# Vision tower on one core: prologue order, value stages of two attentions, and the class token's scale

## The reference

```
# tokenizer: 128 images, a 9x9 grid of 14x14x3 patches in 9 windows of 3x3 patches
pe   = conv(pixel_values, conv_w)                     # 81 patches x 256
red  = mean of pe over the 9 patches of a window
q    = layernorm(red)*g+b @ la_wq ; k, v = layernorm(pe)*g+b @ la_wkv
local= red + softmax(q k * scale) v @ la_proj_w + la_proj_b       # one query, 9 keys
cls  = class_emb + softmax(gq gk * scale) gv @ ga_proj_w + ga_proj_b   # 9 windows as keys
h    = concat(local @ mod_w + mod_b, cls)             # 10 tokens an image
# attention 0 (16 heads of 16, 10 tokens, two scores masked), mixture of experts,
# attention 1 (causal over 10 tokens, scores clipped), low-rank block:
h = h + attention0(layernorm(h)) ; h = h + experts(layernorm(h))
h = h + attention1(layernorm(h)) ; h = h + lowrank(layernorm(h))
```

## Time and profile before

| | us |
|---|---|
| median of 3 runs | 852.29 (847.16 to 853.2) |
| the profiled execution | 849.13 |
| its span | 847.4 |
| mean granted clock of PE, share of full | 0.931 |
| busy: PE, DVE, ACT, POOL | 729.8, 535.9, 358.6, 396.5 |

### The profile page before, as it was taken

How to read it: one execution, slowest core, us unless ns; L and a number is a source line. 1 busy time by engine, 2 the same in 40 slices (tenths; PEclk the granted TensorE clock), 3 DMA queues, 4 the chain that set the end, 5 groups by cost and what they waited for, 6 DMA issues and landing times.

```text
span 847.4 us, 13115 instructions
## 1 busy us (share of the span) xinstructions
PE 729.8 (86%) x4399; PEld 630.6 (74%) x4399; DVE 535.9 (63%) x1253; ACT 358.6 (42%) x904; POOL 396.5 (47%) x272
## 2 busy tenths in 40 slices
PE   2879999999999999996846755999999999595668
PEld 2869998988989887553645754999999999354666
DVE  1578787777777777678999653222222223679956
ACT  3465666656656555532010131444444444162131
POOL 4565767667576661548564202333334332147410
PEclk9899999999999999999958865999999999597999
DMA  8532222222222020000020047799989980400001
GB/s 257 174 91 81 86 87 86 81 60 76 87 86 84 4 100 1 0 1 0 1 100 1 26 174 298 239 339 325 332 331 331 330 327 28 160 0 2 0 1 63
DMA packets 34489, 102.76 MB, mean 121 GB/s; under 512 B 3624, under 2 KB 12152, under 8 KB 27000
## 3 DMA queue, kind: packets, MB, share of 16 engines
q1 hardware_dynamic: 31832, 94.84, 32.6%
q0 software_dynamic: 2592, 7.10, 2.2%
HBM read 95.75 MB, written 6.17 MB: 120 GB/s over the span
## 4 chain that ended last, share of the span: by engine, by line
PE 69%; DVE 20%; POOL 3%; DMA 2%; issue 2%; ACT 1%; SPq 1%; POOLq 1%; DVEq 0%; ACTq 0%
PE banks L1581 12%; PE banks L1589 11%; PE banks L287 10%; PE banks L289 10%; PE banks L288 10%; PE banks L294 6%; PE banks L300 4%; DVE a_prod L1158 4%; PE banks L1260 4%; DVE a_o L1469 2%; DVE a_s L1393 2%; DVE banks L1393 1%; DVE w_raw L1402 1%; PE banks L1290 1%; PE banks L1919 1%
## 5 line engine op out<-in xcount | busy, mean ns | idle before, releaser
L401 POOL TENSOR_TENSOR x_lo<-xraw,x_hi 128x640 fp32r<-128x640 f32 x81 | 129.3, 1603 | 109.8 <-ACT x_hi L395 109.8
L287 PE MATMUL banks<-wc_hi,x_hi 128*128 128x256 f32 x405 | 121.9, 301 | 17.9 <-POOL x_lo L401 12.6
L1679 ACT ACTIVATE hid<-banks,b 128x128 f32<-128x128 f32 x216 | 79.3, 367 | 110.0 <-PE banks L1581 110.0
L288 PE MATMUL banks<-wc_lo,x_hi 128*128 128x256 f32 x405 | 116.5, 288 | 0.0
L289 PE MATMUL banks<-wc_hi,x_lo 128*128 128x256 f32 x405 | 116.4, 287 | 0.0
L287 PEld LDWEIGHTS banks<-wc_hi,x_hi 128*128 128x128 f32 x405 | 79.5, 196 | 20.4 <-issue 12.9
L1838 DVE TENSOR_TENSOR res<-banks,xb 128x256 f32<-128x256 f32 x27 | 11.5, 425 | 127.2 <-PE banks L1589 127.2
L288 PEld LDWEIGHTS banks<-wc_lo,x_hi 128*128 128x128 f32 x405 | 79.7, 197 | 1.8 <-issue 0.2
L289 PEld LDWEIGHTS banks<-wc_hi,x_lo 128*128 128x128 f32 x405 | 79.3, 196 | 0.0
L424 DVE BATCH_NORM_STATS2 stats<-banks 128x6 f32<-128x256 f32 x81 | 34.6, 427 | 69.7 <-ACT pe_sb L418 69.0
L418 ACT ACTIVATE pe_sb<-banks 128x256 f32<-128x256 f32 x81 | 31.0, 383 | 111.8 <-PE banks L289 111.8
(11 more groups left out here) (298 smaller groups left out, 1778.5 us busy)
## 6 DMA issues: line engine op xcount, KB each, us to landing
w_raw<-in_w SPq DMA_DIRECT2D x28, 1024.0 KB, 6.7
xraw<-in_x_main SPq DMA_DIRECT2D x27, 768.0 KB
w1more<-in_w SPq DMA_DIRECT2D x13, 1024.0 KB, 5.8
w2more<-in_w SPq DMA_DIRECT2D x13, 1024.0 KB, 8.2
xraw<-in_x_rest SPq DMA_DIRECT2D x27, 114.0 KB
yl<-y_rows SPq DMA_DIRECT2D x2, 1028.0 KB, 7.1
a_w<-in_qkv_w SPq DMA_DIRECT2D x2, 768.0 KB, 5.4
x_rows<-w_raw SPq DMA_DIRECT2D x5, 256.0 KB, 2.0
```

The costliest lines, as they stand in the source:

```text
L287: pe.matmul(dst, a[0], b[0], start=start, stop=False)
L288: pe.matmul(dst, a[0], b[1], start=False, stop=False)
L401: pool.tensor_tensor(x_lo[:, i % RING_X, :], xraw[:, k].rearrange("p c b -> p (c b)"), x_hi[:, i % RING_X, :], ALU.subtract).then_inc(sem( ...
L1679: act.activation(hid[:, s % 2, fc, :], bank(fc % 2, 0, P), ACT.Gelu, bias=b1[:, bass.ds(e * FC + fc, 1)]).then_inc(sem("gelu_made"), 1)
```

## The change

- SP issues the first third of the first window, `vecs`, `wkv`, and then the other two thirds; `rows` moves behind them and is counted with the other weights (112 becomes 128). DVE's wait before the bias columns asks for `vecs` and `wkv` alone.
- PE's product of the bias columns moves from behind patch 5 to behind patch 1, the turn from 7 to 4; ACT's split of the weights from 8 to 5; DVE scales them behind `measure(1)`. POOL's first inverse root moves from behind `x_lo` 7 to 6. Normalizing patches 0 and 1 and turning patch 0 move ahead of the end of the loop (ACT at i = 10, 11; PE ahead of the last `conv`).
- Attention 0's class token: the maximum of its scores is kept in PSUM; DVE's product of score row 7 moves ahead of the wait for the projected class token; DVE subtracts the mean before POOL's inverse root is there, and ACT multiplies by the root alone.
- Value stages: ACT writes the values again with the key as the inner axis (`spread_values`: layer 0 in one instruction of 2560 elements behind the exponentials, layer 1 one of 256 elements for each tile). DVE's product reads these and writes in the same order, all through one slot. POOL folds a row of more than 5 keys: a second instruction adds the upper keys onto the lower ones (5 of 5 rows in layer 0, rows 6 and 8 in layer 1), and PE sums 5 keys instead of 10 (4 or 5 instead of 7 and 9).
- h is added by PE (one more identity product behind `project_o`'s), ACT copies the sum to h, and `add_o` keeps only the statistics.

```diff
@@ lower_scores
+            top_score = smax[:, :] if n < NW else bank(6, C, C + H8)
+            link(dve.tensor_reduce(top_score, by_head(sc), AX, ALU.max))
+            dve.tensor_tensor(by_key(sc), by_key(sc), over_keys(top_score), ALU.subtract).then_inc(sem("score_made"), 1)
@@ act_end
-            norm_x(act, 0, 9)
+            act.wait_ge(sem("rstd_made"), batch_of("attention 0", 3)[0] + 1)
+            act.wait_ge(sem("a_turned"), NW - 1)
+            act.activation(a_xn[:, NW % 2, :], agg[:, :], ACT.Identity, scale=rstd[2][:, NW:NW + 1]).then_inc(sem("a_xn_made"), 1)
@@ dve_end
             pool_sums(dve, link, 0, 5)
+            row_product(dve, 0, 7)
             dve.wait_ge(sem("proj_done"), NW + 1)
...
-            shift_of(dve, *batch_of("attention 0", 3))
+            dve.tensor_scalar(agg[:, :], h_at(NW), mv[2][:, NW, 0:1], None, ALU.subtract).then_inc(sem("nmr_made"), 1)
             pool_sums(dve, link, 0, 6)
-            for t in range(7, T):
+            row_sum(dve, link, 0, 7)
+            for t in range(8, T):
@@ value products
+        def kept_keys(layer, t):
+            n = keys(layer, t)
+            return (n + 1) // 2 if n > HALF else n
+        def fold_pool_values(pool, layer, t):
+            n, m = keys(layer, t), kept_keys(layer, t)
+            slot = pool_slot(layer, t)
+            return pool.tensor_tensor(slot[:, 0:(n - m) * C], slot[:, 0:(n - m) * C], slot[:, m * C:n * C], ALU.add)
+        def values_by_channel(n=T):
+            return a_prod[:, 1, :].rearrange("p (c s) -> p c s", s=T)[:, :, 0:n]
+        def dve_values(dve, layer, t):
...
+            return dve.tensor_tensor(a_prod[:, 0, 0:n * C].rearrange("p (h d s) -> p h d s", h=H16, s=n),
+                                     values_by_channel(n).rearrange("p (h d) s -> p h d s", d=D16),
+                                     p_t.unsqueeze(2).broadcast_to([P, H16, D16, n]), ALU.mult)
@@ pool_attention
+                if folded(layer, t):
+                    pool_values(pool, layer, t).then_inc(sem("unfolded"), 1)
+                    pool.wait_ge(sem("unfolded"), NW + 1 + made)
+                    fold_pool_values(pool, layer, t).then_inc(sem("a_pool_values_made"), 1)
@@ pe_attention: turn_o, project_o
-                ns, slot = keys(layer, t), pool_slot(layer, t)
+                ns, slot = kept_keys(layer, t), pool_slot(layer, t)
...
-                mm_rows(pe, bank(6 + t % 2), a_oT[:, t % 2, :], wo, 0, C).then_inc(sem("a_o_done"), 1)
+                for c in range(CH):
+                    pe.matmul(bank(6 + t % 2), a_oT[:, t % 2, c * P:(c + 1) * P], wo[:, c, :], start=(c == 0), stop=False)
+                pe.matmul(bank(6 + t % 2), ident[:, :], h_at(t), start=False, stop=True).then_inc(sem("a_o_done"), 1)
@@ act_attention
+        def spread_values(act, layer, a, b):
+            act.wait_ge(sem("a_qkv_made"), seen(layer, "qkv_made", 2 * b))
+            act.activation(values_by_channel()[:, :, a:b].rearrange("p c s -> p s c"), a_qkv[:, a:b, 2 * C:3 * C], ACT.Copy)\
+               .then_inc(sem("a_values_spread"), 1)
+        def copy_h(act, layer, t):
+            act.wait_ge(sem("a_o_done"), seen(layer, "o_done", t + 1))
+            act.activation(h_at(t), bank(6 + t % 2), ACT.Copy).then_inc(sem("a_h_made"), 1)
@@ add_o
-            dve.wait_ge(sem("a_o_done"), seen(layer, "o_done", t + 1))
-            dve.tensor_tensor(h_at(t), bank(6 + t % 2), h_at(t), ALU.add).then_inc(sem("a_h_made"), 1)
@@ sync
+            load_x(sp, 0, 0, first=True)
+            sp.dma_start(vecs[:, :], d["vecs"]).then_inc(sem("wkv_loaded"), 16)
+            sp.dma_start(wkv_raw[:, :, :], two("la_wkv")).then_inc(sem("wkv_loaded"), 16)
+            for g in range(1, NP // GRP):
                 load_x(sp, 0, g, first=True)
-            sp.dma_start(rows[:, :], d["rows"].broadcast_to([P, len(ROWS) * C])).then_inc(sem("wkv_loaded"), 16)
+            sp.dma_start(rows[:, :], d["rows"].broadcast_to([P, len(ROWS) * C])).then_inc(sem("tok_w_loaded"), 16)
@@ vector, prologue
-            dve.wait_ge(sem("wkv_loaded"), 48)
+            dve.wait_ge(sem("wkv_loaded"), 32)
```

More of the change, by code:

```diff
@@ L1215, in pool_attention @@
                     pool.wait_ge(sem("a_o_turned"), seen(layer, "o_turned", POOL_VALUES[layer][i - 2] + 1))
-                value_products(pool, layer, t, pool_slot(layer, t)[:, 0:n * C].rearrange("p (s h d) -> p s h d", s=n, d=D16))\
-                    .then_inc(sem("a_pool_values_made"), 1)
+                made = sum(folded(0, q) for q in POOL_VALUES[0]) * layer + sum(folded(layer, q) for q in POOL_VALUES[layer][:i + 1])
+                if folded(layer, t):
+                    pool_values(pool, layer, t).then_inc(sem("unfolded"), 1)
+                    pool.wait_ge(sem("unfolded"), NW + 1 + made)
+                    fold_pool_values(pool, layer, t).then_inc(sem("a_pool_values_made"), 1)
+                else:
+                    pool_values(pool, layer, t).then_inc(sem("a_pool_values_made"), 1)
             if layer == 0:
@@ L1350, in act_attention @@
                         copy_qkv(act, 1, t - 1)
-                    if t >= 4:
-                        row_exponent(act, SCORED[t - 4])
+                        spread_values(act, 1, t - 1, t)
+                    if t >= 5:
+                        row_exponent(act, SCORED[t - 5])
                 copy_qkv(act, 1, T - 1)
-                for t in SCORED[T - 4:]:
+                for t in SCORED[T - 5:T - 2]:
+                    row_exponent(act, t)
+                spread_values(act, 1, T - 1, T)
+                for t in SCORED[T - 2:]:
                     row_exponent(act, t)
@@ L2141, in _ @@
             link = Chain(dve, "link")
-            for i in range(EARLY_KEYS):
+            for i in range(2):
                 measure(dve, i)
-            early_variances(dve, 0)
             dve.wait_ge(sem("kvb_done"), 1)
@@ L2150, in _ @@
                    .then_inc(sem("wkv_scaled"), 1)
[L2151 removed]
+            for i in range(2, EARLY_KEYS):
                 measure(dve, i)
[L2153 removed]
+            early_variances(dve, 0)
             dve.wait_ge(sem("wkv_hi_made"), CH)
@@ L2157, in _ @@
                    .then_inc(sem("wkv_lo_made"), 1)
-            measure(dve, 8)
+            for i in range(EARLY_KEYS, 7):
+                measure(dve, i)
+            shift_of(dve, 0, 0, EARLY_KEYS)
+            for i in range(7, NP):
+                measure(dve, i)
             late_variances(dve, 0)
-            measure(dve, 9)
+            measure(dve, NP)
+            dve.wait_ge(sem("tok_w_loaded"), 128)
             tile_stats(dve, "class", 0, rows[:, 3 * C:4 * C])
```

88 lines of the change are left out of this document (45 added, 43 removed).

## The result

The changed kernel took 821.9 us (median of 4 runs, 819.8 to 825.99) beside 850.87 of the kernel before on the same chip: a ratio of 0.9674, 95% interval 0.9641 to 0.9707. The forecast was 819 (811 to 831) and faster. The profiled execution took 819.8 us, 29.3 less than the 849.1 of before; the sum of the forecast was 30.6.

What follows compares the result with a forecast made beforehand. PE is nearly full in rounds and experts, so only thin stretches can shrink: 5.2 (prologue) + 3.4 (class token) + 12 (attention 0) + 10 (attention 1) = 30.6 off 849.1 gives 818.5, stated as 819 us, range 811 to 831.

Steps and rivals of the forecast that it cites:

- Prologue, 5.2: Before the rounds: reordered steps start PE's first projection at 46.5 instead of 51.7; gain 5.2 us, from 2 to 8.
- The sum over POOL's queue: Prologue: from the first root at 29.2, splits, waits, roots, class shift and split product add up to 46.5.
- PE's stop before patch 7: Prologue: DVE's split of the weights (2.7 us) ahead of `measure(5)` holds patch 7 to about 31.5.
- Class token, 3.4: Attention 0's class token: early subtraction lets ACT start at about 398 instead of 401.2; gain 3.4 us, from 1 to 5.6.
- The rival of the held subtraction: Class token: POOL's next product makes the subtraction wait 3.4 us, so that gain is gone; 822, chance 0.05.
- Attention 0, 12: Attention 0's values: faster DVE products, folds and fewer PE products end the stage at 476.5, not 488.57; gain 12 us, 9 to 14.
- The rival of the slow product: Value stages: the weights' PSUM broadcast keeps DVE's product at 4.72 us; gains 8.5 and 6.5; 825, chance 0.10.
- Attention 1, 10: Attention 1's values: ACT starts the low-rank block at 808.8 instead of 818.75; gain 10 us, from 7.5 to 11.5.
- projections whose copies have some 1 to 2 us to spare: 0: Attention 1: ACT's ten spreads, 0.65 us each, fit beside the projections and cost 0.
- the rival of the cold PE: Value stages: PE, idle some 2.5 us before each POOL row, runs slow; about 2 us a stage, 823, chance 0.12.
- The slower rival: Value stages: POOL's folds cost more than they save, from 7.1 us a fold; 856 at 8 us, chance 0.02.
- its least gain: Whole kernel: the lowest gains of all four parts together, 19.5 us, giving 833.

Runs made afterwards that it cites:

- x_max_sbuf: Changed kernel with the class token's maximum over its scores kept in SBUF as before, not in PSUM: 822.6 us, ratio 0.9668.
- x_no_fold: Changed kernel without POOL's folds, PE adding all keys of a row: 821.5 us, ratio 0.9651.
- x_late_spread: Changed kernel with ACT's attention 1 spreads moved behind the last copy and the exponents one tile earlier: 820.4 us, ratio 0.964.
- x_warm: Changed kernel with idle PE products, whose results nothing reads, added ahead of both value stages: 821.4 us, ratio 0.9665.
- x_class_before: Changed kernel with the class token's part as before: shift for subtraction, row 7's product not pulled ahead, maximum in SBUF: 824.7 us, ratio 0.9705.

## Why the prediction was right

- **Prologue, 5.2: measured 5.08, and 4.8 by undoing it.** The sum over POOL's queue held step by step: first root done at 30.07 (forecast 29.2), second begun at 41.08 (40.8), class shift 1.49, PE at 46.64 (46.5). One step on the way was wrong and cost nothing: PE's stop before patch 7 came at 31.73 but was for POOL's `x_lo`, not for DVE's `measure(5)`, since DVE's split of the weights took 1.28 us, not 2.7.
- **Class token, 3.4: measured 3.37, twice.** Its steps stand: the subtraction took 0.34, DVE waited 2.93 us (2.5) for POOL's product of column 8, and the maximum's place was worth 0 with PE's projections as its cover, by the run that changed it alone. The rival of the held subtraction fell: 0.34 us.
- **Attention 0, 12: measured 12.56 to the norm, 13.9 to the gather.** Product 2.82 as forecast, fold 2.89 (2.95), spread 4.76 (4.8), row of POOL 7.67 (7.8). What was not in the sum is the 1.38 us behind the norm: the router's products of 8 columns took 0.51 us instead of 0.86 while the clock was still up. That is the clock's, and not surely the change's: x_max_sbuf, with the same code there, had them at 0.86 and N-G at 25.81, as before. The rival of the slow product fell with 2.81. What the forecast missed is what the fold was worth: it never worked the stage out without it. When I did, ahead of that run, I took 8.1 us a pair for PE and the fold as worth 5 us. PE does a pair in 7.28 us, and the fold's 7.65 makes attention 0 longer by 1.1. The sum was right; the fold's part in it was a loss.
- **Attention 1, 10: measured 7.5** (8.53 of values, less 0.75 of scores and 0.25 at the end). The step that failed is "projections whose copies have some 1 to 2 us to spare: 0". The spreads took 0.67 us each (0.65 forecast), but DVE then waited 1.55 us for a copy, and S-V1 was 0.75 us longer. In both runs that take the spreads out of the loop it is back at 34.81 and 34.80, in one of them with the exponents' table load (1.28 us) left in its later place, so the cost is the spreads'. The other 1.2 us is the rival of the cold PE, in a place I had not thought of: not at POOL's rows with folds, but at row 0's projection, where it held up the slot of POOL's row 4. With the clock up the stage took 24.54 to 24.56 us from DVE's first product to ACT; the forecast had 24.35.
- **The slower rival** (folds of 7.1 us or more) fell with 2.89. Rounds and experts kept their length, 0.19 and 0.15 us aside.

The sum was 1 us over what the span showed, and the median lies 2.1 above the profiled execution of the changed kernel, as it did by 3.2 for the kernel before. Part of that closeness is luck: attention 1 fell 2.5 us short, and the 1.4 us behind attention 0, which were not in the sum, made up for half of it. The range had a slip too: its least gain was turned into a time with the 3.2 us of the median (833), its greatest without (810 instead of 813).

## What to carry to other kernels

Before moving work from one engine to another, add up the pace of each engine per pair of rows for both arrangements, with all other parts of the change made. Here, in attention 0, folding five keys gave 7.65 us (GpSimd), none 7.28 (TensorE) and three 6.6 (GpSimd, with DVE level). The middle way, priced like this, gained 2.5 us where the change's own fold lost 1.1. After a gain, look at which small instructions now fall beside the other engine's long ones: an addition to four numbers grew from 1.02 to 3.07 us and took nearly half of what the faster stage gave. And let what PE waits for go first on the engine that makes it, then follow the next wait: the first move brought the start 6 us forward, and 2.6 of them stayed.

## What the hardware showed beyond that

**The clock doesn't follow the program alone.** Up to C the code of x_no_fold, x_late_spread and x_warm is that of the changed kernel, word for word, yet A-C is 50.8 us in them and 49.1 in the others. The windows of the changed kernel and of x_class_before, which shares the fall, and PE's last stop and the first product that the fall hits, in both:

```profile
345.00:350.00 5.00, 4.03 (x14) 2.23 (x14) 3.99 (x10) 2.54 (x7) 0.45 (x1) 1.00 0.00 0
```

```profile
345.00:350.00 5.00, 4.04 (x10) 1.85 (x11) 3.92 (x9) 1.93 (x6) 0.46 (x1) 0.76 0.00 0
```

```profile
345.97 0.44 PE L300 MATMUL banks<-ident,agg 128*128 128x128 f32 x2 [1.40 <-DVE agg L615]
346.99 1.98 PE L1285 MATMUL banks<-a_w,a_xT 128*128 128x512 f32 x4
```

```profile
345.96 0.44 PE L300 MATMUL banks<-ident,agg 128*128 128x128 f32 x2 [1.41 <-DVE agg L615]
346.98 3.20 PE L1281 MATMUL banks<-a_w,a_xT 128*128 128x512 f32 x4
```

From 339.5 to 347 PE's instructions in the two traces start within 0.02 us of each other, the stop of 1.4 us among them, and yet the clock stays up in the one and falls in the other; 1.7 us follow from it. Of the 13 profiles of the changed kernel and its variants four have this fall. F-A (296.9 to 298.2 with the same prologue) goes with how soon the clock comes back in the first round: from 50 to 54 us it is 1.00 in the changed kernel and 0.69 in x_max_sbuf, whose F-A is 1.2 longer. N-G (24.2 to 24.9, once 25.8) and V1-Z (24.5 to 24.6, or 25.4 to 25.9) are told above. Such differences come to some 3 us between profiles of the same code, and may well be what the runs of one kernel differ by: the four of the changed kernel took 819.8 and 819.9 at a mean clock of 0.941, 823.9 and 826.0 at 0.933 and 0.930. What decides a fall was not found.

**ACT pays for writes 10 words apart.** The spread took 4.76 us for 2560 elements, 1.86 ns each, and the small ones 0.67 us for 256, where a copy of 256 consecutive words out of PSUM takes 0.38. The forecast's slope from the exponentials, 1.78, held for a plain copy: from 256 to 2560 elements it is 1.78.

**Some of DVE's small instructions end with GpSimd's running one, and others don't.** Held were shifts of one and of five numbers (1.49 and 3.37 us, 0.13 to 0.17 when free), additions of a constant to four numbers (1.02 and 3.07), and a subtraction of 72 elements from SBUF (2.32). Of these the last was freed by one operand in PSUM (0.23); on the others that was not tried. Not held, in the changed kernel, though they began and ended inside a GpSimd instruction on tensors: 43 ends of statistics at 0.17 to 0.18 us, the statistics themselves at 0.39 to 0.43, reductions, reciprocals of 8 numbers at 0.20, and additions of a constant to a single number, seven of them at 0.15.
